# Stacked q and k of five head groups by DMA through DRAM scratch, expert weights in seven loads

## What is computed

```python
ys = y * scale                                   # condition, one vector per sequence
d = rsqrt(einsum('bi,io->bo', ys * ys, weight * weight) + EPS)
xc = einsum('bsi,io->bso', x * ys[:, None, :], weight) * d[:, None, :]
q, k, v = split(xc @ w_qkv.T)                    # 16 heads of 8 features
q, k = rope(q), rope(k)
scores = einsum('bhsd,bhtd->bhst', q, k) / sqrt(8)     # causal
x = x + (softmax(scores) @ v) @ w_out.T
x2 = (shared experts(x) + top-2 of 8 routed experts(x)) / 4
x = x + x2 + top-3 of 8 zones(x2)                # each zone: gelu(. @ Wa[e]) @ Wb[e]
```

## Time and profile before

| | us |
|---|---|
| median of 3 runs (208.48 to 210.38) | 208.83 |
| the profiled execution | 209.39 |
| its span, first to last instruction | 207.7 |
| TensorE matmul busy | 187.0 |
| VectorE busy | 151.0 |
| ScalarE busy | 147.5 |
| GpSimd busy | 93.8 |
| mean granted TensorE clock | 0.981 of full |

### The profile page before, as it was taken

The page is one execution under the profiler, slowest core; times in us unless marked ns, Lnnn a source line. Parts: engine busy times, 40 slices in busy tenths (PEclk is TensorE's granted clock), DMA queues, the critical chain, the costliest instruction groups (busy, mean ns, idle before and its releaser), DMA issues.

```text
span 207.7 us, 3357 instructions
## 1 busy us (share of the span) xinstructions
PE 187.0 (90%) x1016; PEld 129.3 (62%) x1016; DVE 151.0 (73%) x455; ACT 147.5 (71%) x245; POOL 93.8 (45%) x101
## 2 busy tenths in 40 slices
PE   7994999999999988998999899894999689979993
PEld 3753756666666656654565567783677467747881
DVE  4584789888888885895048756599789957698752
ACT  4487758587878767878852876735769679868880
POOL 4625078351436333752521675834268920585000
PEclk9998899999999999999999999999699999999999
DMA  5602331239523224232011229950000000001001
GB/s 157 210 0 51 86 76 34 51 88 349 169 64 92 69 82 114 67 116 76 3 51 52 57 56 333 340 140 0 0 3 2 0 0 0 2 3 51 0 0 51
DMA packets 9793, 16.06 MB, mean 77 GB/s; under 512 B 2208, under 2 KB 3360, under 8 KB 9648
## 3 DMA queue, kind: packets, MB, share of 16 engines
q1 hardware_dynamic: 9200, 15.46, 24.8%
q10 hardware_dynamic: 576, 0.39, 0.6%
HBM read 9.23 MB, written 2.69 MB: 57 GB/s over the span
## 4 chain that ended last, share of the span: by engine, by line
PE 55%; DVE 19%; ACT 11%; issue 6%; DMA 3%; POOL 2%; DVEq 1%; SPq 1%; ACTq 0%; POOLq 0%
PE psum L1211 8%; PE psum L1262 7%; PE psum L1321 7%; DVE t_q_pad L727 6%; PE psum L1242 5%; PE psum L1323 5%; PE psum L1322 5%; ACT t_q_pad L931 3%; DVE psum L569 3%; DMA t_q_pad<-t_stacked 3%; PE psum L1245 2%; PE psum L1134 2%; PE psum L1079 2%; PE psum L1194 2%; DVE t_raw L713 1%
## 5 line engine op out<-in xcount | busy, mean ns | idle before, releaser
L569 DVE CUSTOM_DVE_ANT_0 psum<-psum,t_causal 128x128 f32<-128x128 f32 (+3 forms) x128 | 59.5, 522 | 15.5 <-PE psum L1211 14.9
L883 ACT ACTIVATE t_probs<-psum 128x768 f32<-128x768 f32 (+1 forms) x48 | 41.2, 882 | 4.0 <-PE psum L1242 3.0
L931 ACT CAST t_q_pad<-t_raw 128x512 fp32r<-128x512 f32 x48 | 29.6, 618 | 13.7 <-DVE t_raw L713 8.3
L1211 PE MATMUL psum<-t_stacked,t_q_pad 128*128 128x256 f32 (+2 forms) x128 | 37.0, 361 | 0.8 <-ACT t_q_pad L830 0.2
L918 ACT ACTIVATE t_raw<-psum 128x512 f32<-128x512 f32 x48 | 28.6, 595 | 9.2 <-PE psum L1357 4.1
L474 POOL TENSOR_SCALAR_AFFINE_SELECT t_probs<-t_probs 128x512 f32<-128x512 f32 x32 | 19.9, 635 | 32.5 <-ACT t_probs L883 32.5
L727 DVE TENSOR_TENSOR t_q_pad<-t_raw,t_q_pad 128x512 fp32r<-128x512 f32 x32 | 27.6, 880 | 8.4 <-ACT t_q_pad L931 8.4
L1211 PEld LDWEIGHTS psum<-t_stacked,t_q_pad 128*128 128x128 f32 x128 | 21.9, 190 | 14.2 <-DVE t_row_max L569 9.7
L502 POOL TENSOR_TENSOR t_q_pad<-t_raw,t_q_pad 128x512 fp32r<-128x512 f32 x16 | 20.9, 1316 | 21.3 <-ACT t_q_pad L931 17.8
L1262 PE MATMUL psum<-t_probs,t_v_all 128*32 128x512 f32 (+3 forms) x256 | 20.5, 439 | 0.0
L1242 PE MATMUL psum<-t_q_mov,t_k_pad 128*128 128x512 f32 (+1 forms) x64 | 18.3, 371 | 0.2
(11 more groups left out here) (200 smaller groups left out, 397.4 us busy)
## 6 DMA issues: line engine op xcount, KB each, us to landing
t_k_pad<-t_stacked SPq DMA_DIRECT2D x32, 64.0 KB, 2.0
scratch<-t_o_sb SPq DMA_DIRECT2D x8, 256.0 KB, 2.0
t_probs<-in_L_ffn_Wa SPq DMA_DIRECT2D x2, 1024.0 KB, 8.2
t_q_pad<-t_stacked SPq DMA_DIRECT2D x28, 64.0 KB, 2.0
t_raw<-in_experts SPq DMA_DIRECT2D x1, 1792.0 KB, 8.7
...
```

Of the source, the lines that this page charges most:

```text
L569: last = V.tensor_tensor_reduce(scores, scores, causal[:, S - width:S], 1.0, 3 * BIG, ALU.add, ALU.max, row_max[s][:, qb, j:j + 1])
L883: A.activation(probs[s][:, c, 2 * h2:2 * h2 + 2, 0:w], ST[:, slot_of("exp", n, u):slot_of("exp", n, u) + 2, 0:w], ACT.Exp, scale=float(1.0 ...
L931: A.copy(h_hi[r], src_).then_inc(hi_done, 1)
L1211: last = T.matmul(ring("max", n, u)[:, i * 2 * P:i * 2 * P + width], q_pad[s][:, j, qb * P:(qb + 1) * P], stacked[:, 2 * n + 1, 0:width], ...
```

## The change

Groups 0 to 2 are stacked as before (BY_PE = 3). For groups 3 to 7 the selection matmuls and the ScalarE copies are gone. SyncE writes qk_hi and qk_lo of those groups' heads into ten more slots of `scratch` in the stacked layout (`spill`, three DMAs for q and three for k: of the 32 partitions of group 3 before the loop, of all 128 partitions of sequence 1 in interval 0), and block 0 of all five groups from the first 8 partitions of stacked q and stacked k of group 0, each row written 20 times (`spill_rest`, one DMA for q, one for k). `load_stacked(n)` loads a stacked k and q (256 KB each), and `pad_q` and `pad_k` of groups 3 to 7 read DRAM in place of SBUF. What overwrites qk_hi and qk_lo waits on `spilled`. The exponentials' units alternate over ST without a stack between them. The expert weights come in seven loads of 512 columns after store_sums(1) to store_sums(4) (EXPERT_LOADS), their splits each move one group later, and invert(0) and normalise(0) move to units 80 and 93.

```diff
@@ -46,11 +46,11 @@
 LEAD, FIRST = 8, 3
-STACK_IN = {0: 3, 1: 4, 2: 5, 3: 6, 4: 7}
+BY_PE = 3
+SPILLS = 6
 ST_ORDER = [("stack", 2), ("project", 1)]
 for _n in range(GROUPS):
-    ST_ORDER += [("exp", _n, _u) for _u in range(4)] + ([("stack", STACK_IN[_n])] if _n in STACK_IN else [])
-    ST_ORDER += [("exp", _n, 4), ("exp", _n, 5)]
+    ST_ORDER += [("exp", _n, _u) for _u in range(STU)]
@@ -102,8 +102,9 @@
-INV_AT = [78, 88]
-SPLITS = {(2, 0): 0, (2, 2): 1, (3, 0): 2, (3, 2): 3, (4, 0): 4, (4, 2): 5, (5, 0): 6}
+INV_AT = [80, 93]
+SPLITS = {(3, 0): 0, (3, 2): 1, (4, 0): 2, (4, 2): 3, (5, 0): 4, (5, 2): 5, (6, 0): 6}
+EXPERT_LOADS = [(), (0, 1), (2, 3), (4, 5), (6,), (), (), ()]
@@ -274,8 +275,10 @@
         q_padded = [sem(f"q_padded{s}") for s in range(2)]
         k_padded = [sem(f"k_padded{s}") for s in range(2)]
+        ld_stack = {n: sem(f"ld_stack{n}") for n in range(BY_PE, GROUPS)}
         stored = [sem(f"stored{s}") for s in range(2)]
         xc_ready = [sem(f"xc_ready{k}") for k in range(3)]
+        ld_raw = [sem(f"ld_raw{k}") for k in range(len(SPLITS))]
         block = ctx.enter_context(nc.Block())
@@ -310,6 +313,16 @@
             return psum[:, ((6, 7), (4, 5))[h][i], 0:S2]
+        def laid(n, i):
+            return scratch[GROUPS + 1 + i * (GROUPS - BY_PE) + n - BY_PE]
+        def laid_blocks(b, i):
+            first = GROUPS + 1 + i * (GROUPS - BY_PE) + (NG - BY_PE if b else 0)
+            slots = scratch[first:first + (NG if b else NG - BY_PE)]
+            return slots.rearrange("g (j r d) t -> r (g j) d t", j=HG, r=KB)
@@ -336,27 +349,63 @@
                 s = n % 2
-                sp.wait_ge(rep_copied, 3 if n == 1 else 2 * n + 3)
+                if n < BY_PE:
+                    sp.wait_ge(rep_copied, 3 if n == 1 else 2 * n + 3)
                 if n >= 2:
...
                 for j in range(HG):
                     q = slice(32 * j, 32 * j + 32)
-                    sp.dma_start(f32_of(q_pad[s][q, j, :]), f32_of(stacked[q, 2 * n, :])).then_inc(q_padded[s], 16)
+                    src = f32_of(stacked[q, 2 * n, :]) if n < BY_PE else laid(n, 0)[q, :]
+                    sp.dma_start(f32_of(q_pad[s][q, j, :]), src).then_inc(q_padded[s], 16)
...
                 s = n % 2
-                sp.wait_ge(rep_copied, (2, 4)[n] if n < 2 else 2 * n + 4)
+                if n < BY_PE:
+                    sp.wait_ge(rep_copied, (2, 4)[n] if n < 2 else 2 * n + 4)
                 if n >= 2:
...
                 for j in range(HG):
                     q = slice(32 * j, 32 * j + 32)
-                    sp.dma_start(f32_of(k_pad[s][q, j, :]), f32_of(stacked[q, 2 * n + 1, :])).then_inc(k_padded[s], 16)
+                    src = f32_of(stacked[q, 2 * n + 1, :]) if n < BY_PE else laid(n, 1)[q, :]
+                    sp.dma_start(f32_of(k_pad[s][q, j, :]), src).then_inc(k_padded[s], 16)
+            def spill(b, i):
+                q = slice(0, P) if b else slice(32 * BY_PE, P)
+                sp.wait_ge(hi_ready, 4 * b + (i + 1 if b else 3 + i))
+                for r in ((1, 2), (1, 3))[i]:
+                    sp.dma_start(laid_blocks(b, i)[r], f32_of(qk_hi[q, i, :])).then_inc(spilled, 16)
+                sp.wait_ge(lo_ready, 4 * b + (i + 1 if b else 3 + i))
+                sp.dma_start(laid_blocks(b, i)[(3, 2)[i]], f32_of(qk_lo[q, i, :])).then_inc(spilled, 16)
+            def spill_rest():
+                sp.wait_ge(rep_copied, 6)
+                for i in range(2):
+                    first = GROUPS + 1 + i * (GROUPS - BY_PE)
+                    slots = scratch[first:first + GROUPS - BY_PE]
+                    rows = slots.rearrange("g (j r d) t -> r d (g j) t", j=HG, r=KB)[0]
+                    sp.dma_start(rows, f32_of(stacked[0:HD, i, :]).unsqueeze(1).broadcast_to(
+                        [HD, (GROUPS - BY_PE) * HG, S])).then_inc(rest_rows, 16)
+            def load_stacked(n):
+                for i in (1, 0):
+                    sp.dma_start(f32_of(stacked[:, 2 * n + i, :]), laid(n, i)).then_inc(ld_stack[n], 16)
...
                 sp.wait_ge(pv_copied, n + 1)
                 sp.dma_start(scratch[n], o_sb[n % 2][:]).then_inc(stored[n % 2], 16)
+            def load_experts(k):
+                c = slice(k * S, (k + 1) * S)
+                if k == 0:
+                    sp.wait_ge(v_ready, B)
+                    sp.wait_ge(roped_ready, 6)
+                sp.dma_start(raw[:, c], io["experts"][:, c]).then_inc(ld_raw[k], 16)
@@ -381,24 +430,33 @@
             sp.wait_ge(pad1_zero, 1)
             pad_q(1)
+            spill(0, 0)
+            spill(0, 1)
+            spill_rest()
             sp.dma_start(small[:], io["small"]).then_inc(ld_small, 16)
...
             pad_q(2)
             pad_k(1)
+            sp.wait_ge(rest_rows, 16 * 2)
+            sp.wait_ge(spilled, 16 * SPILLS)
             for n in range(GROUPS):
+                if n == 1:
+                    sp.wait_ge(spilled, 2 * 16 * SPILLS)
                 if n + 3 < GROUPS:
+                    load_stacked(n + 3)
                     pad_q(n + 3)
+                if n == 0:
+                    spill(1, 0)
                 if n + 2 < GROUPS:
                     pad_k(n + 2)
+                if n == 0:
+                    spill(1, 1)
                 if n == NG:
                     spread_inverse(0)
                 store_sums(n)
-                if n == 0:
-                    sp.wait_ge(v_ready, B)
-                    sp.wait_ge(roped_ready, 6)
-                    sp.dma_start(raw[:], io["experts"]).then_inc(ld_raw, 16)
+                for k in EXPERT_LOADS[n]:
+                    load_experts(k)
                 if n == NG - 1:
@@ -429,7 +487,7 @@
             pool.wait_ge(dvar_ready, 1)
             G.tensor_tensor(dinv[:], dvar[:], dexp[:], ALU.pow).then_inc(dinv_ready, 1)
-            for g in range(2, NG):
+            for g in range(2, BY_PE):
                 G.memset(f32_of(sel[:, g, :, :]), 0.0).then_inc(sel_zero, 1)
@@ -481,14 +539,15 @@
                         pool.wait_ge(hi_ready, 4 + c)
-                        pool.wait_ge(rep_ready, 2 * NG + 2)
+                        pool.wait_ge(rep_ready, 2 * BY_PE + 2)
+                        pool.wait_ge(spilled, 16 * SPILLS)
                         G.tensor_tensor(qk_lo[:, c - 1, :], roped[:, c - 1, :], f32_of(qk_hi[:, c - 1, :]),
...
                 if n == NG:
-                    pool.wait_ge(rep_ready, 2 * GROUPS + 2)
+                    pool.wait_ge(rep_ready, 2 * BY_PE + 2)
                     G.memset(f32_of(sel_e), 0.0).then_inc(sele_zero, 1)
@@ -821,7 +880,8 @@
             def take_hi(i):
                 act.wait_ge(roped_ready, 4 + i + 1)
-                act.wait_ge(rep_ready, 2 * NG + 2)
+                act.wait_ge(rep_ready, 2 * BY_PE + 2)
+                act.wait_ge(spilled, 16 * SPILLS)
                 A.copy(qk_hi[:, i, :], roped[:, i, :]).then_inc(hi_ready, 1)
@@ -865,7 +925,7 @@
                 if w == 3:
                     act.wait_ge(const_ready, 1)
-                bank = psum[:, (2, 3, 4, 5)[w - 2], :] if w < 6 else ST[:, slot_of("stack", w // 2) + i, :]
+                bank = psum[:, (2, 3, 4, 5)[w - 2], :]
                 if i == 0:
@@ -967,10 +1027,9 @@
                 hi, lo, c, at_ = chunks[k]
-                if k == 0:
-                    act.wait_ge(ld_raw, 16)
+                act.wait_ge(ld_raw[k], 16)
                 if k == UP_COLS // S:
-                    act.wait_ge(rep_ready, 2 * GROUPS + 2)
+                    act.wait_ge(spilled, 2 * 16 * SPILLS)
                 A.copy(hi[:, c:c + S], raw[:, at_:at_ + S]).then_inc(w_hi, 1)
@@ -1011,14 +1070,9 @@
                     copy_pv(n - 1)
                 exp(n, 2)
-                if n == 0:
-                    take_sel(3)
                 if (n, 0) in SPLITS:
                     split_high(SPLITS[n, 0])
                 exp(n, 3)
-                if n in STACK_IN:
-                    copy_stacked(2 * STACK_IN[n])
-                    copy_stacked(2 * STACK_IN[n] + 1)
                 if n == GROUPS - 1:
@@ -1175,22 +1229,15 @@
             def stack(w):
-                b, g, i = w // (2 * NG), w // 2 % NG, w % 2
-                if b == 0 and i == 0:
+                g, i = divmod(w, 2)
+                if i == 0:
                     pe.wait_ge(sel_ready, g + 1)
-                if b and w % (2 * NG) < 2:
-                    pe.wait_ge(lo_ready, 4 + i + 1)
-                if w < 6:
-                    bank = psum[:, (2, 3, 4, 5)[w - 2], :]
-                    if w == 2:
-                        pe.wait_ge(pj_copied, 1)
-                    if w == 4:
-                        pe.wait_ge(q0_placed, 2 * HG)
-                        pe.wait_ge(rep_copied, 6)
-                else:
-                    bank = ST[:, slot_of("stack", w // 2) + i, :]
-                    if i == 0:
-                        wait_slot("stack", w // 2)
+                bank = psum[:, (2, 3, 4, 5)[w - 2], :]
+                if w == 2:
```

(22 more changed lines are left out.)

3 lines of the change are left out of this document (removed).

## The result

The changed kernel takes 213.39 us (median of 4 runs, 212.80 to 213.71) against 209.61 us (208.48 to 210.71) for the kernel before in the same comparison: 1.018 times as long, with a 95% interval of 1.011 to 1.025, so it is slower beyond the noise. The profiled execution took 213.71 us, its span is 212.0, the mean granted clock 0.96. The forecast was 211.9, range 204.4 to 213.9, slower as the likeliest.

A forecast was written before the change was run, and what follows sets the result against it. TensorE's matmul side, 90% busy, was taken as nearly full; 209.39 - 4.14 (selections gone) + 6.9 (group 2's q late) + 0.3 (group 7's q) = 212.45, or 211.9 us on the median's scale; range 204.4 to 213.9.

The forecast's parts named there:

- Intervals two to six: Attention stage, between copies of q into q_mov: with selections gone, about 11.1, 9.0, 9.0, 9.0 and 9.2 us.
- The knot: Fifth interval: split_high(4) overwrites hi parts, so ScalarE waits for the last selection and TensorE for ScalarE; 1.39 us saved.
- Seventh interval: Attention stage: splits 5 and 6 move here between exponentials TensorE waits for; 0.8 us lost, bounds 0 and 1.2.
- q of group 7: SyncE's queue: issued about 2 us before use, behind a store, expert loads and stacked loads; 0.3 us lost, bounds 0 and 1.
- The rest's rate: Before the loop: 320 rows out of 8 partitions at 62 GB/s take 10.6 us, so group 2's q lands at 41.3.
- SyncE's issue: Queue before the loop: about 0.6 us a DMA, so pad_q(2) is issued by 31.7 to 33.2.
- Half clock: After TensorE's idle wait for group 2's q: 1.95 us of work slows; 1.2 us added, bounds 0 and 1.9.
- Behind attention: Stages after the last copy into q_mov: the forecast had no term for a saving there.
- The loads: Experts' weights: no one waits for their data, in one load or seven; no cost or gain.
- A: Rest rows before the loop cost 0.0875 us each, group 2's q lands by 34 to 35; faster, 205.0 us; chance 0.29.
- B: Attention intervals: VectorE stays the pace through the ring of three banks, savings covered; 208.5 us; chance with C 0.13.
- C: SyncE's queue is the bound in attention intervals; at 1 us above, three times, 208; folded into B, together 0.13.

The follow-up runs named there:

- the version without stacking: Kernel before with everything of the change but the stacking: seven expert loads, SPLITS one group later, INV_AT at 80 and 93; 206.38 us, ratio 0.985.
- the rest from DRAM: Changed kernel with the two rest DMAs reading the 320 rows from a DRAM constant instead of 8 partitions of stacked; 203.44 us, ratio 0.970.
- SPLITS alone: Kernel before with only the table SPLITS moved one group later, selections and ScalarE copies kept; 208.53 us, ratio 0.994.
- INV_AT added: Kernel before with SPLITS one group later and INV_AT at 80 and 93, experts' weights still in one load; 207.47 us, ratio 0.993.
- the probe: Kernel before with five late DMAs, each after the last landed, writing 160 rows from different partitions of v_all into DRAM; 209.79 us (one run).
- the two runs with probes: Kernel before with added DMAs out of v_all: four back to back after group 5's store, 209.73 us; five one at a time late, 209.79 us.
- the order alone: Changed kernel with group 2's q pads and group 1's k pads ahead of the rest DMAs, small and gate_rows in SyncE's queue; 212.75 us (one run).

## Why the forecast was right, and where it was off

The direction, the place and the pattern held; 211.9 was 1.5 us under. By its steps, on the scale of the profiled executions (209.39 to 213.71, 4.3 us):

- **Intervals two to six.** Forecast 11.1, 9.0, 9.0, 9.0, 9.2; measured 11.2, 8.9, 9.0, 9.0, 9.2. The difference of two paths from place_max to the laying gave the selections' price to a few hundredths in three intervals of four. From the version without stacking to the one with the rest from DRAM, both with seven loads, the second to fifth intervals fall by 0.73, 0.69, 0.95 and 0.95 us. So the third interval owes 0.7 us to the stacking, not 0.95.
- **The knot.** Forecast 1.39, measured 1.40 by SPLITS alone. But it is not the stacking's: moving a table does it.
- **Seventh interval.** Forecast 9.3, measured 8.5. The step that failed is the reading that only the splits count there. SPLITS alone did cost 1.03 us; the change of INV_AT, which the forecast did not price, gave it back.
- **q of group 7.** Forecast 0.3 lost, and the sixth interval is 9.24, as before. It is there all the same: TensorE's weight load waits 0.7 us for q_pad, and with all but the stacking the interval is 8.96. The tables took 0.2 off it (9.18 with SPLITS alone, 8.97 with INV_AT added), which the forecast had left out, and the late q gave it back.
- **The rest's rate.** This is the term that was mis-sized most. The forecast took 10.6 us, from 62 GB/s out of 8 partitions, scaled from the pads. Measured are 49 to 50 GB/s, 13.1 to 13.4 us for the 655 KB. The row scaled from was too cheap: 32 neighbours cost 0.15 us a row in the probe, against 0.132 in the pads' window; why the pads show less is open. The estimate by the Trainium skill ("SBUF — State Buffer", section "Door 1: The DMA port swizzle"), 12.0 us, was nearer than mine and also short.
- **SyncE's issue.** The second failed step: that the queue issues at 0.6 us a DMA whatever the engines do. The last of group 2's q pads was issued at 42.48, against 31.7 to 33.2 in the forecast. Most of that wait costs nothing, since the slow transfer ran until about 41 anyway, 2 us and a little more behind the 38.9 of the forecast. But q came at 44.35, not 41.3, 3.1 us later; what the rate does not explain, under 1 us, is the stall's.
- **Half clock.** From q to the laying 3.4 us were measured, 3.15 forecast. The clock was still down at the copy behind it, 1.33 us after the laying in place of 0.78, 0.55 us more. In all 10.9 us lost where 6.9 were forecast.
- **Behind attention.** Forecast nothing, measured 1.5 us saved. The stretch takes 108.7 us before and 108.1 and 108.6 in the two runs with probes; 108.1 with SPLITS alone, 107.8 with INV_AT added, 106.8 with the seven loads added; 107.0 with stacking by DMA, INV_AT and one load. So it is not the stacking's, since it is there without it. In one of the runs with the changed kernel's code there, the one with the order alone, it is 105.8 against 107.1, so single executions differ by up to 1.3 us; which edit gives the rest stays open.
- **The loads.** "No one waits for the experts' data, in one load or seven" is true of the data, but does not make the loads free: what stands behind one load waits, and with the stacked rows coming by DMA that is 6 us. The seven loads are what lets the new layout work.

The sum thus held in part by luck, because two misses cancelled: 4.0 us too little for the first interval, 2.6 us too little saved (0.8 in the seventh, 0.3 in the sixth, and 1.5 behind attention). Rivals: A's price of a row is wrong here; its time for cheap rows, 205.0, is near the 203.4 with the rest from DRAM. B is excluded, since TensorE is the pace in the intervals after the first, with VectorE at 8.0 of 8.9 us. C is excluded too: the only later wait for a q that lengthens an interval is group 7's, by 0.3 us.

So the change is three things: stacking by DMA saves about 3 us (203.4 against 206.4 without it), the tables and loads about 3 (206.4 against 209.4), and reading the rest rows out of 8 partitions costs 10. The first two hang together: with one load, stacking by DMA takes 209.5 us and stacking by TensorE 207.5, so the layout saves only with its loads in parts.
